# Attention scores in halves through three PSUM tiles and maxima unit by unit through three, on one Trainium2 core

## The reference, cut to what matters

```python
# layer 0, "attn_a" (NH=16, HD=8, D_R=32)
scores = einsum('bqhd,bkhd->bhqk', q, k) + einsum('bqr,bkr->bqk', q_rope, k_rope)[:, None]
w = softmax(where(causal, -inf, scores / sqrt(HD + D_R)), axis=-1)
attn = einsum('bhqk,bkhd->bqhd', w, v).reshape(B, T, D_MODEL)
# layer 1, "attn_a" (H=16, HD=64, a latent of LD=32)
attn = softmax(where(mask, einsum('bqhd,bkhd->bhqk', q, k) / sqrt(HD), neg_inf), axis=-1)
y = einsum('bhqk,bkhd->bqhd', attn, v)
```

## Time and profile before

| | us |
|---|---|
| median of 3 runs (3158.69, 3158.78, 3168.52) | 3158.78 |
| the profiled execution, its own time | 3168.43 |
| its span, first to last instruction | 3166.7 |
| TensorE busy | 2361.7 |
| VectorE busy | 1743.7 |
| ScalarE busy | 1241.0 |

### The profile page before, as it was taken

How to read it: one execution, slowest core, us unless ns; L and a number is a source line. 1 busy time by engine, 2 the same in 40 slices (tenths; PEclk the granted TensorE clock), 3 DMA queues, 4 the chain that set the end, 5 groups by cost and what they waited for, 6 DMA issues and landing times. The chain is left out here.

```text
span 3166.7 us, 46665 instructions
## 1 busy us (share of the span) xinstructions
PE 2361.7 (75%) x13512; PEld 1225.4 (39%) x13512; DVE 1743.7 (55%) x5508; ACT 1241.0 (39%) x1983; POOL 488.8 (15%) x524
## 2 busy tenths in 40 slices
PE   4559999999956328866999999999677292877382
PEld 1114344343334126532443434444254271554262
DVE  4656666666344886265665655666365324576223
ACT  2405455555534644553444444444222141343141
POOL 1400000000003000032000000000043463033554
PEclk9759999999977659877999999999888596988686
DMA  4272444443030000233122121121120152000144
GB/s 130 76 144 45 86 76 85 86 85 60 11 103 3 1 8 28 64 110 109 44 57 54 45 55 42 48 64 37 60 83 21 52 142 81 3 4 15 40 138 129
DMA packets 177903, 199.81 MB, mean 63 GB/s; under 512 B 36384, under 2 KB 117920, under 8 KB 177568
## 3 DMA queue, kind: packets, MB, share of 16 engines
q1 hardware_dynamic: 160000, 173.72, 22.1%
q0 software_dynamic: 9216, 19.02, 1.8%
q10 hardware_dynamic: 8448, 4.20, 0.4%
HBM read 127.09 MB, written 69.76 MB: 62 GB/s over the span
## 5 line engine op out<-in xcount | busy, mean ns | idle before, releaser
L910 ACT ACTIVATE at_probs<-at_score 128x1024 f32<-128x1024 f32 (+7 forms) x1024 | 655.2, 652 | 872.8 <-PE at_score L835 539.1
L935 DVE CUSTOM_DVE_ANT_0 at_masked<-at_mx,g_maskw 128x512 bf16<-128x512 f32 (+3 forms) x1024 | 483.4, 486 | 180.9 <-PE at_mx L801 177.6
L801 PE MATMUL at_mx<-at_K,at_Q 96*128 96x512 bf16 (+7 forms) x1536 | 467.0, 344 | 119.0 <-DVE at_mpart L935 40.9
L833 PE MATMUL at_score<-at_Q,at_K 96*128 96x512 bf16 (+7 forms) x1536 | 504.1, 332 | 28.9 <-issue 14.3
L835 PE MATMUL at_score<-at_Q,at_K 98*128 98x512 bf16 (+7 forms) x1536 | 507.2, 331 | 0.0
L931 DVE TENSOR_REDUCE at_mpart<-at_mx 128x1 f32<-128x512 f32 x512 | 353.8, 691 | 265.3 <-PE at_mx L801 245.1
L855 PE MATMUL at_outp<-at_probs,at_vop 128*32 128x512 f32 (+6 forms) x3072 | 445.2, 497 | 0.0
L801 PEld LDWEIGHTS at_mx<-at_K,at_Q 120*128 120x128 bf16 (+1 forms) x1536 | 148.4, 98 | 440.3 <-DVE at_mpart L935 198.6
L833 PEld LDWEIGHTS at_score<-at_Q,at_K 120*128 120x128 bf16 (+1 forms) x1536 | 149.8, 98 | 339.3 <-issue 183.1
L1025 POOL MEMSET n_spread<- 16x128 f32 (+1 forms) x2 | 0.7, 356 | 1541.0 <-POOLq L636 1541.0
L838 PE MATMUL at_score<-g_maskkq,g_identb 128*128 128x128 bf16 x1024 | 225.3, 220 | 0.0
(11 more groups left out here) (467 smaller groups left out, 3408.6 us busy)
## 6 DMA issues: line engine op xcount, KB each, us to landing
at_Q<-q SPq DMA_DIRECT2D x192, 128.0 KB, 3.0
at_Q<-qr SPq DMA_DIRECT2D x72, 256.0 KB, 5.9
at_K<-kr SPq DMA_DIRECT2D x72, 256.0 KB, 6.9
q<-p_pieces SPq DMA_DIRECT2D x40, 384.0 KB, 3.3
at_K<-k SPq DMA_DIRECT2D x168, 64.0 KB, 2.1
buf<-g_zeros SPq DMA_DIRECT2D x32, 325.0 KB, 5.0
o<-at_osb SPq DMA_DIRECT2D x64, 128.0 KB
n_oc<-o SPq DMA_DIRECT2D x8, 1024.0 KB, 5.0
```

Of the source, the lines that this page charges most:

```text
L801: pe.matmul(bank[:, 0:hi - lo], Q0[0:R, g % 4, j, qt * P:(qt + 1) * P], K0[0:R, g % 4, j % KG, lo:hi], start=True, stop=True).then_inc(s_m ...
L833: pe.matmul(bank, K0[0:R0, g % 4, j % KG, kb * P:(kb + 1) * P], Q0[0:R0, g % 4, j, lo:hi], start=True, stop=False)
L910: act.activation(probs[:, kb % 2, j, kb * P:T], src, ACT.Exp, scale=cf.scale).then_inc(s_exp, 1)
L935: dve.tensor_tensor_reduce(masked[:, u % 2, 0:w], mx[:, u % 2, 0:w], k.maskw[:, CH - w:CH], 1.0, NEG, ALU.add, ALU.max, mpart[:, part, j, ...
```

## The change

Scores: the unit becomes one half of one head. Three `score` tiles of one bank stand in place of two of two banks, and ScalarE takes one exponential per half, so 12 per head where there were 8. Maxima: three `mx` tiles in place of two. In `kb` 0 to 3 one wide unit follows each half of scores; the narrow units go one at a time, the first after `values(3)`, one behind each head of `kb` 5 to 7, and the last `G-1` after `values(7)`. The shift: the partial maxima `mpart` are transposed as they are, in fp32, both parts; only then does VectorE combine, negate and split them, four operations on `G*8` partitions by 128 columns, the maximum and its reads in PSUM. `turn_max` waits for the reductions alone; the three `mx` tiles come back together at the end. Part 1 of blocks 0 to 3 is filled with -1e30 once.

```diff
-    U = QT * G
-    MU = 12 * G + 2
-    NARROW = {5: [3], 6: [2, 1], 7: [0]}
-    WIDE = {0: [7], 1: [6], 2: [5], 3: [4]}
+    SB, MB = 3, 3
+    U = 12 * G
+    MU = 12 * G + MB
+    NARROW = [(qt, 0, j) for qt in (3, 2, 1, 0) for j in range(G)]
+    WIDE = [(qt, part, j) for qt in (7, 6, 5, 4) for j in range(G) for part in range(2)]
     NARROW_U, WIDE_U = 4 * G, 8 * G
     NPC = 8 * 4
+    def halves(kb):
+        return [0, 1] if kb < 4 else [1]
+    def half_units(kb):
+        return G * (2 * kb if kb < 4 else 4 + kb)
...
-        masked = c.sb("masked", [P, 2, CH], BF16)
-        score = c.ps("score", [P, 2, 2, CH])
+        masked = c.sb("masked", [P, MB, CH], BF16)
+        score = c.ps("score", [P, SB, CH])
         outp = c.ps("outp", [P, 2, CH])
-        mx = c.ps("mx", [P, 2, CH])
+        mx = c.ps("mx", [P, MB, CH])
...
+            def turn_max(b, g):
                 n = b * GN + g
+                u = NARROW_U + WIDE_U
+                pe.wait_ge(s_mxf, n * MU + u + MB)
+                for part in range(2):
+                    pe.transpose(mx[0:G * QT, (u + part) % MB, 0:P], mpart[:, part, :, :].rearrange("p j q -> p (j q)"),
+                                 k.ident[:]).then_inc(s_mx, 1 + part * (MB - 2))
...
-            def scores(b, g, kb, j):
+            def scores(b, g, kb, j, half):
                 n = b * GN + g
+                h = half_units(kb) + len(halves(kb)) * j + halves(kb).index(half)
+                pe.wait_ge(s_exp, n * U + h + 1)
+                lo, hi = max(half * CH, kb * P), (half + 1) * CH
+                diag = lo == kb * P
+                bank = score[:, h % SB, lo - half * CH:CH]
+                R0, R1 = cf.rows
+                pe.matmul(bank, K0[0:R0, g % 4, j % KG, kb * P:(kb + 1) * P], Q0[0:R0, g % 4, j, lo:hi],
+                          start=True, stop=False)
+                last = pe.matmul(bank, K1[0:R1, g % 2, j % KG, kb * P:(kb + 1) * P], Q1[0:R1, g % 2, j, lo:hi],
+                                 start=False, stop=not diag)
+                if diag:
+                    last = pe.matmul(bank[:, 0:P], k.identb[:], k.maskkq[:], start=False, stop=True)
                 last.then_inc(s_st, 1)
...
-                u1, u2 = NARROW_U, 0
+                wide = iter(enumerate(WIDE))
+                narrow = iter(enumerate(NARROW))
+                def next_wide():
+                    i, unit = next(wide)
+                    if one:
+                        max_unit(*one, unit, NARROW_U + i)
+                def next_narrow():
+                    i, unit = next(narrow, (None, None))
+                    if two and unit:
+                        max_unit(*two, unit, i)
                 for kb in range(QT):
-                    if kb == 5 and two:
+                    if kb == 4 and two:
                         await_rows0(*two)
                     for j in range(G):
-                        scores(b, g, kb, j)
-                        if kb in WIDE and one:
-                            u1 = max_units(*one, WIDE[kb], j, u1)
-                        if kb in NARROW and two:
-                            u2 = max_units(*two, NARROW[kb], j, u2)
+                        for half in halves(kb):
+                            scores(b, g, kb, j, half)
+                            if kb < 4:
+                                next_wide()
+                        if kb > 4:
+                            next_narrow()
                     if kb == 4 and one:
-                        turn_max(*one, u1)
+                        turn_max(*one)
                     if kb > 0:
                         values(b, g, kb - 1)
+                    if kb == 4:
+                        next_narrow()
                 values(b, g, QT - 1)
+                for _ in range(G - 1):
+                    next_narrow()
...
-                        u = kb * G + j
-                        act.wait_ge(s_st, n * U + u + 1)
-                        src = score[:, u % 2, :, :].rearrange("p h t -> p (h t)")[:, kb * P:T]
-                        act.activation(probs[:, kb % 2, j, kb * P:T], src, ACT.Exp,
-                                       scale=cf.scale).then_inc(s_exp, 1)
+                        for half in halves(kb):
+                            h = half_units(kb) + len(halves(kb)) * j + halves(kb).index(half)
+                            lo, hi = max(half * CH, kb * P), (half + 1) * CH
+                            act.wait_ge(s_st, n * U + h + 1)
+                            act.activation(probs[:, kb % 2, j, lo:hi], score[:, h % SB, lo - half * CH:CH], ACT.Exp,
+                                           scale=cf.scale).then_inc(s_exp, 1)
...
+            def finish_max(b, g):
                 n = b * GN + g
+                u = NARROW_U + WIDE_U
+                parts = [mx[0:G * QT, (u + part) % MB, 0:P] for part in range(2)]
+                larger = mx[0:G * QT, u % MB, P:2 * P]
+                dve.wait_ge(s_mx, n * MU + u + MB)
+                dve.tensor_copy(first[:], parts[0]).then_inc(s_mc, 1)
+                dve.wait_ge(s_mc, 3 * n + 1)
+                dve.tensor_tensor(larger, parts[1], first[:], ALU.max).then_inc(s_mc, 1)
+                dve.wait_ge(s_mc, 3 * n + 2)
+                dve.tensor_scalar(mrow[:, 0, :], larger, -1.0, None, ALU.mult).then_inc(s_mc, 1)
+                dve.wait_ge(s_mc, 3 * n + 3)
+                dve.scalar_tensor_tensor(mrow[:, 1, :], larger, -1.0, mrow[:, 0, :], ALU.mult,
+                                         ALU.subtract).then_inc(s_mrow, 2)
+                dve.wait_ge(s_mrow, 2 * n + 2)
+                dve.sem_inc(s_mxf, MB)
```

More of the change, by code:

```diff
@@ L790, in _, with max_unit @@
         def _(pe):
-            def max_units(b, g, qts, j, u):
+            def max_unit(b, g, unit, u):
+                qt, part, j = unit
                 n = b * GN + g
                 R = cf.rows[0]
[L795 to L806, removed]
-                n = b * GN + g
[L809 to L813, removed]
+                lo, hi = part * CH, min((qt + 1) * P, (part + 1) * CH)
+                pe.wait_ge(s_mxf, n * MU + u + 1)
+                pe.matmul(mx[:, u % MB, 0:hi - lo], Q0[0:R, g % 4, j, qt * P:(qt + 1) * P],
+                          K0[0:R, g % 4, j % KG, lo:hi], start=True, stop=True).then_inc(s_mx, 1)
+            def turn_max(b, g):
+                n = b * GN + g
+                u = NARROW_U + WIDE_U
[3 more added lines that the diff above has]
+                                 k.ident[:]).then_inc(s_mx, 1 + part * (MB - 2))
             def await_rows0(b, g):
@@ L818, in await_rows0 @@
                     pe.wait_ge(s_s0[g % 4], 16 * nsh * (b + 1))
-            def scores(b, g, kb, j):
+            def scores(b, g, kb, j, half):
                 n = b * GN + g
-                u = kb * G + j
[L825 to L829, removed]
-                    diag = lo == kb * P
-                    bank = score[:, u % 2, half, lo - half * CH:CH]
-                    R0, R1 = cf.rows
-                    pe.matmul(bank, K0[0:R0, g % 4, j % KG, kb * P:(kb + 1) * P], Q0[0:R0, g % 4, j, lo:hi],
-                              start=True, stop=False)
-                    last = pe.matmul(bank, K1[0:R1, g % 2, j % KG, kb * P:(kb + 1) * P], Q1[0:R1, g % 2, j, lo:hi],
-                                     start=False, stop=not diag)
-                    if diag:
-                        last = pe.matmul(bank[:, 0:P], k.identb[:], k.maskkq[:], start=False, stop=True)
+                h = half_units(kb) + len(halves(kb)) * j + halves(kb).index(half)
[10 more added lines that the diff above has]
+                    last = pe.matmul(bank[:, 0:P], k.identb[:], k.maskkq[:], start=False, stop=True)
                 last.then_inc(s_st, 1)
@@ L858, in values, with all_max_units @@
                 last.then_inc(s_pv, 1)
-            def all_max_units(b, g, parts, u):
-                for qts in parts.values():
-                    for j in range(G):
-                        u = max_units(b, g, qts, j, u)
-                return u
+            def all_max_units(b, g, units, u):
+                for i, unit in enumerate(units):
+                    max_unit(b, g, unit, u + i)
+            pe.wait_ge(s_filled, 1)
             await_rows0(0, 0)
-            all_max_units(0, 0, WIDE, all_max_units(0, 0, NARROW, 0))
-            turn_max(0, 0, NARROW_U + WIDE_U)
+            all_max_units(0, 0, NARROW, 0)
+            all_max_units(0, 0, WIDE, NARROW_U)
+            turn_max(0, 0)
             await_rows0(0, 1)
@@ L898, in _ @@
         def _(act):
-            act.sem_inc(s_exp, 2)
+            act.sem_inc(s_exp, SB)
             def step(b, g):
```

64 lines of the change are left out of this document (19 added, 45 removed).

## The result

The changed kernel takes **3051.5 us** (median of 4 runs, 3046.1 to 3054.8), the kernel before 3160.1 beside it: a ratio of 0.9649, with a 95% interval of 0.9625 to 0.9674. The profiled execution took 3054.7 us with a span of 3052.9, against 3166.7. Forecast were 3057 and a range of 3025 to 3100.

The account below looks back on a forecast made before the run. TensorE was taken as the bound, standing still 5.3 and 2.1 us per group. Gains 57 + 3.5 + 39 + 1 + 5 - 4 = 102 us, off the median of 3158.8, gave 3057 us; range 3025 to 3100.

Parts of the forecast that it names:

- loop ends: Four branches at loop ends: 3.5 us idle stays, the slower clock afterwards costs a full TensorE 1 us each, -4.
- call 0, period without narrow units: Next to last period of call 0, where narrow maxima units have run out: gain 3.5 us.
- call 1, before the first score: 1457.38 to 1480.32 us: with three tiles VectorE runs without gaps, 17.4 us for 22.9, gain 5.
- TensorE's own work: TensorE's steps per group: 35.05 of 40.4 us in call 0, 22.3 of 24.4 in call 1; only the rest can be won.
- Units and three tiles, no stall from `kb` 0 to 3: Maxima units one by one between halves of scores: VectorE faster than TensorE in each stage, so no stall.
- VectorE's 0.61 us from unit to unit: VectorE starts its next maxima unit 0.61 us after one of 512 columns, so pairs take 1.21 us at `kb` 0.
- the rival at 3107 us: VectorE becomes the bound: units start only after the one before ends, 0.69 + 0.03 apart; 50 us back; chance 0.09.
- The chain: Four dependent VectorE operations behind the turn, 1.32 us, hold the maxima tiles: new TensorE stall of 0.48 us per group.
- The group's start: VectorE has narrow units, copy and `vop` before the first wide unit: 0.35 us left in call 0, 0.12 in call 1.
- The last group: Last period of call 0, without maxima: gain 0, as TensorE alone was taken to fill it.
- TensorE alone, 27 us of steps: Reason given for no gain in call 0's last period: TensorE's own steps there make 27 us.
- Costed at nothing: Exponentials per half, 32 to 48 per group of four heads: no cost; 1.1 us per group if ScalarE were the limit.

Follow-up runs that it names:

- the kernel with both stalls away: Changed kernel with the turn in its old order (combine, negate, split before bf16 transposes) and the group's closing copy on ScalarE: 3024.1 us.
- pairs through three tiles: Changed kernel with interleaving undone: both wide units of a head follow its two halves, narrow units at their old places: 3055.7 us.

## Why the prediction was right

Term by term, in us of the span, against 113.8 measured between the two profiled executions (108.6 between the medians); the prediction's -4 for loop ends is put with the periods they lie in:

| | forecast | measured |
|---|---|---|
| call 0, first copy to 14th | 57 - 2 | 536.2 - 481.4 = 54.8 |
| call 0, period without narrow units | 3.5 | 3.8 |
| call 0, last period | 0 | 2.7 |
| call 0, first score to first copy | not counted | 42.7 - 38.2 = 4.5 |
| call 1, 29 periods | 39 - 2 | 39.4 |
| call 1, last two periods | 1 | 1.7 |
| call 1, first score to first copy | not counted | 0.9 |
| call 1, before the first score | 5 | 4.2 |
| the rest | 0 | 1.8 |

- **TensorE's own work** (35.05 and 22.3 us) held: the kernel with both stalls away runs at 35.14 and 22.48 (with two bf16 transposes, as in that sum). This is the step that carried the forecast.
- **Units and three tiles, no stall from `kb` 0 to 3**: right at `kb` 1 to 3. That taking turns was part of the reason was all but wrong: pairs through three tiles lose 0.2 us. The stall of the kernel before was read as about 0.1 per head in each of `kb` 0 to 3; by the table of stages it was 0.14 at `kb` 2 and 0.22 at `kb` 3. Nothing hung on it, since the gain was taken from the whole period.
- **VectorE's 0.61 us from unit to unit**: 0.60 measured, with a unit of 0.69, and not the 0.72 of the rival at 3107 us. The Trainium skill ("VectorE: DVE Perf Modes", section on the DRAIN) says that the next operation waits until the pipe is empty and adds that one that is not held starts earlier; the trace agrees with what it adds.
- **The chain**: 0.48 forecast (its own terms, 1.67 - 1.22, give 0.45), 0.30 measured. Its operations took 0.28 each as worked out (1.30 for 1.32). What was over-sized is what lies around them: 0.11 us from the start of the matmul behind the transposes to the first operation and 0.12 behind the last, not 0.2 and 0.15.
- **The group's start**: 0.35 and 0.12 forecast, 0.64 and 0.18 measured. This was the term without a sum behind it, "I leave", and the one most off in call 0. Per group it was 0.29 and 0.06 too little, the chain 0.18 too much, so the two together missed by 0.1 in call 0 and hid each other, which is luck.
- **The last group, 0 forecast, 2.7 measured**: the step "TensorE alone, 27 us of steps" took a period of 31.2 for a busy TensorE. It was a stall on the score ring: 35.9, 28.4 and 27.3 us with two, three and four half tiles, and 29.4 with four but one exponential for both halves. So three half tiles with an exponential each are worth more than two whole ones, and still short of four by 1.1 us where no maxima run between. "Costed at nothing" was right for the plain groups only.
- **The first groups** were left out of the sum, 5.4 us.
- **Loop ends**: -1 each was forecast. In call 0 they cost 4.7 and 4.9 us over a plain period, where the kernel before had 5.7, so they gave 1.9; in call 1 6.8 and 7.1 where it had 5.9 and 6.0, so they took 2.0. Two profiles of the same kernel differ there by up to 2 us, so this stays open. The close 54.8 for 55 in the table is luck: the plain groups of call 0 give 4.07 us each (means of 40.37 and 36.30) and not 4.4, 4 us less over 13, and the loop ends make up for it.
- **The shift**: slack of 2.6 us was right (4.2 us more cost 1.4). The price beyond it, one microsecond each, was set too low: it leaves out the clock behind a stop.

The omissions (8 us, the last group of call 0 and the first groups) were all on one side; the forecast lay 5.5 us high.

## What to carry to other kernels

Work out the bounding engine's own steps from start-to-start times before weighing any stall; the difference to the period is all that a reordering can win, and it also says when to stop. When two consumers share PSUM, count tiles per consumer by its pace in the stage where the producer's steps are shortest, and by what happens while it is away (a copy, a dependent chain), not by its mean pace: here the third tile for the one that is waited for, paid with the fourth of the other, was worth some 90 us, the order of the units 4. A dependent chain should not hold tiles that a matmul waits for: run it ahead, on data in SBUF, under work that doesn't need them, or move the matmul behind such work.

## What was not expected of the hardware

- The same [128, 1024] copy out of PSUM takes 1.02 us on ScalarE and 1.23 on VectorE.
- VectorE's operations in the chain take 0.28 us on 32 partitions by 128 columns out of PSUM and 0.17 to 0.19 on 128 partitions by 16 to 32 columns in SBUF, so the four take 1.30 us behind the turn and 0.83 ahead of it. Columns and memory change together here; which of them makes the difference is not shown.
- A store of the shift lands in 1.3 us in 30 of 32 groups of call 1, but in 1.8 to 5.0 in six of the 16 of call 0, in the same kernel.
- A stop of 3.20 us brought TensorE back at a granted clock of 0.50, with steps of 0.43 us for 0.22, so the delay cost more than its length.
